# Delta-rule and linear-attention loops written out, with a new order of steps and a second set of statistics

## What is computed

```python
def _forward(x, ...):                       # one sequence: 512 x 256
    h = rmsnorm(layernorm(x) * ln1_g + ln1_b)
    q, k, v = (silu(causal_conv4(h @ W)) for W in (Wq, Wk, Wv))
    q, k = l2norm(q) * Kd ** -0.5, l2norm(k)
    g = -exp(A_log) * softplus(h @ Wa + dt_bias); beta = sigmoid(h @ Wb)
    # 4 heads, Kd = 64, Vd = 128, token after token:
    S = S * exp(g_t); S = S + k_t (x) ((v_t - k_t S) * beta_t); o_t = q_t S
    o = rmsnorm(o) * silu(h @ Wg)
    x = x + o @ Wo
    return gelu(layernorm(x) @ W2 + b2) + x
```

## Time and profile before

| what | us |
|---|---|
| runs of the kernel before | 4533.56, 4539.57, 4521.59 |
| median | 4533.56 |
| profiled execution | 4549.05 |
| its span | 4547.4 |
| TensorE, VectorE, ScalarE, GpSimd busy in the span | 3962.4, 2468.9, 1990.0, 1100.5 |

### The profile page before, as it was taken

The page is one execution under the profiler, slowest core; times in us unless marked ns, Lnnn a source line. Parts: engine busy times, 40 slices in busy tenths (PEclk is TensorE's granted clock), DMA queues, the critical chain, the costliest instruction groups (busy, mean ns, idle before and its releaser), DMA issues.

```text
span 4547.4 us, 72522 instructions
## 1 busy us (share of the span) xinstructions
PE 3962.4 (87%) x23860; PEld 3063.0 (67%) x23860; DVE 2468.9 (54%) x5456; ACT 1990.0 (44%) x4069; POOL 1100.5 (24%) x1686
## 2 busy tenths in 40 slices
PE   6888788598999999994798888888888888879998
PEld 3555555377888888883576666676676677756666
DVE  6888888452222222224577777777777777431111
ACT  5656555111212222122466666666666666432221
POOL 0111111101222222212334444443334343200000
PEclk8888889699999999997799999999999999889999
DMA  1010010254555555552111111111111110011111
GB/s 34 29 42 29 28 40 22 64 147 167 184 183 183 183 183 183 184 181 82 38 35 42 43 43 43 43 43 43 43 42 43 43 43 24 19 58 55 55 55 51
DMA packets 220956, 346.98 MB, mean 76 GB/s; under 512 B 99972, under 2 KB 171908, under 8 KB 202500
## 3 DMA queue, kind: packets, MB, share of 16 engines
q1 hardware_dynamic: 196932, 272.74, 18.9%
q0 software_dynamic: 23760, 71.07, 5.0%
HBM read 276.61 MB, written 68.16 MB: 76 GB/s over the span
## 4 chain that ended last, share of the span: by engine, by line
PE 23%; POOL 8%; issue 8%; DVE 8%; ACT 4%; DMA 2%; SPq 2%; POOLq 0%; DVEq 0%; ACTq 0%
PE gdr_bank L1320 5%; PE gdr_bank L1311 5%; DVE gdr_y L1729 3%; POOL gdr_vblk L1628 2%; PE gdr_bank L2363 2%; POOL gdr_tblk L1626 2%; PE gdr_bank L2375 1%; PE gdr_bank L2240 1%; PE gdr_bank L2359 1%; SPq L1519 1%; POOL gdr_ssq L1616 1%; PE gdr_bank L2408 1%; POOL gdr_orr L1616 1%; POOL gdr_got L1582 1%; POOL gdr_vblk L1623 1%
## 5 line engine op out<-in xcount | busy, mean ns | idle before, releaser
L525 ACT ACTIVATE moe_rel<-moe_fc 128x512 f32<-128x512 f32 x284 | 169.6, 597 | 798.5 <-PE moe_fc L490 798.5
L490 PE MATMUL moe_fc<-moe_xT,moe_win 128*128 128x256 f32 x2272 | 503.8, 380 | 1.5 <-issue 0.8
L501 PE MATMUL moe_o<-moe_wout,moe_hT 128*128 128x256 f32 x2272 | 502.0, 379 | 0.0
L490 PEld LDWEIGHTS moe_fc<-moe_xT,moe_win 128*128 128x128 f32 x2272 | 432.7, 191 | 61.2 <-issue 2.1
L501 PEld LDWEIGHTS moe_o<-moe_wout,moe_hT 128*128 128x128 f32 x2272 | 426.3, 190 | 55.1
L549 DVE TENSOR_TENSOR moe_hT<-moe_rel 128x512 f32<-128x512 f32 x284 | 196.6, 692 | 361.3 <-ACT moe_rel L525 361.3
L1729 DVE SCALAR_TENSOR_TENSOR gdr_y<-gdr_bank,gdr_cw,gdr_y 128x511 f32<-128x511 f32 (+2 forms) x384 | 287.5, 749 | 51.1 <-ACT gdr_y L2007 28.9
L2240 PE MATMUL gdr_bank<-gdr_hT,gdr_wqkv 128*128 128x512 f32 x512 | 263.6, 645 | 31.9 <-ACT gdr_qk L2022 26.8
L558 DVE COPY moe_osb<-moe_o 128x512 f32<-128x512 f32 x71 | 49.1, 692 | 424.9 <-PE moe_o L501 424.9
L2359 PE MATMUL gdr_bank<-gdr_ident,gdr_T 128*128 128x128 f32 x768 | 136.0, 306 | 109.7 <-DMA gdr_T<-blocks_in 95.0
L1311 PE MATMUL gdr_bank<-gdr_hT,gdr_wqkv 128*128 128x512 f32 x512 | 225.4, 599 | 3.5 <-ACT gdr_hT L1329 3.5
(11 more groups left out here) (391 smaller groups left out, 8843.1 us busy)
## 6 DMA issues: line engine op xcount, KB each, us to landing
moe_win<-in_moe_w SPq DMA_DIRECT2D x71, 1024.0 KB, 7.9
moe_wout<-in_moe_w SPq DMA_DIRECT2D x71, 1024.0 KB, 5.1
slots_out<-moe_osb POOLq DMA_DIRECT2D x71, 256.0 KB, 7.4
gdr_fz<-mixed_rows SPq DMA_DIRECT2D x18, 512.0 KB, 3.8
gla_xp<-in_xT_rows SPq DMA_DIRECT2D x16, 512.0 KB, 4.7
gla_xres<-in_x_rows SPq DMA_DIRECT2D x16, 512.0 KB, 3.9
token_rows<-gla_x POOLq DMA_DIRECT2D x16, 512.0 KB, 3.4
rt_W<-in_fc_b SPq DMA_DIRECT2D x32, 256.0 KB, 3.4
```

Of the source, the lines that this page charges most:

```text
L490: ins = nc.tensor.matmul(fc_ps[j][:, m % 2, :], win[u][:, c, m * P:(m + 1) * P], xT[:, c, :], start=(c == 0), stop=(c == DT - 1))
L501: ins = nc.tensor.matmul(o_ps[u][:, t, :], hT[u][:, k, t * P:(t + 1) * P], wout[u][:, k, :], start=(k == 0), stop=(k == FT - 1))
L525: nc.scalar.activation(rel[:, j, :, :], fc_ps[j][:], ACT.Relu).then_inc(relu_done, 1)
```

## The change

The hardware loops of linear attention (VectorE, ScalarE, TensorE) and of the delta rule (all five engines) are written out as Python loops over b=2 to 13, so that every body and period has its own instructions. The slot loops of VectorE, ScalarE and TensorE and `CHUNK_AT` go; each stream has its steps one under the other, in an order that differs in places:

- TensorE: chunk (0,2) ahead of `reach`; the rest of chunk (1,1) and all channel copies of half 1 ahead of `first_half(4,2)` (before: behind it).
- VectorE: `last_sum` from slot 2 to slot 9, between `rates(0)` and `rates(1)`; `last_norm` from slot 4 to slot 13, behind `merge(4,2)` and `merge(4,3)` and ahead of `norm3`; `conv(4)` behind `merge(4,0)` and `merge(4,1)` (before: ahead); the second scan of the second pair behind `merge(6,1)` (before: ahead of `merge(6,0)`).
- ScalarE: `gelu` from slot 0 to behind tap 4, ahead of the half copies of level 4, between `conv_silu(3)` and `conv_silu(4)`; `decay_keys`, `restart`, `squares` and the channel copies by a few places.
- GpSimd: the power for `last_sum` behind the second inversion. SyncE: `return_blocks(1)` ahead of the x3 store.
- `last_sum` and `last_norm` have a third set of `stats`, `agg`, `var` and `rstd`.

```diff
@@ VectorE, linear attention (ScalarE and TensorE alike) @@
-                with dve.Fori(0, (B - 4) // 2) as i:
-                    for u in range(2):
-                        body(i * 2 + 2 + u, u, i * 2 + 1 + u, True, i + 2)
+                for b in range(2, B - 2):
+                    body(b, b % 2, b - 1, True, b // 2 + 1)
@@ delta rule @@
-        stats, agg, var, rstd = ([sb(f"{n}{i}", [P, TT] + w) for i in range(2)]
+        stats, agg, var, rstd = ([sb(f"{n}{i}", [P, TT] + w) for i in range(3)]
...
-            with eng.Fori(0, (B - 4) // 2) as i:
-                for u in range(2):
-                    period(i * 2 + 2 + u, u, here=True, front=True, ln=True, past=True, end=True)
+            for b in range(2, B - 2):
+                period(b, b % 2, here=True, front=True, ln=True, past=True, end=True)
@@ GpSimd @@
-                    if end:
-                        power(b - 2, var[1][:], rstd[1][:], "tl_var", 2, "tl_rstd", TT)
...
                     if here:
                         invert_blocks(1, b)
+                    if end:
+                        power(b - 2, var[2][:], rstd[2][:], "tl_var", 2, "tl_rstd", TT)
@@ VectorE, the new order (conditions left out) @@
+                        merge(4, 0, b)
+                        merge(4, 1, b)
+                        conv(4, b + 1)
...
+                        scan(2, b)
+                        merge(6, 0, b)
+                        merge(6, 1, b)
+                        scan(3, b)
+                        key_decays(1, b)
...
+                        rates(0, b + 1)
+                        last_sum(b - 2)
+                        rates(1, b + 1)
...
+                        merge(4, 2, b)
+                        merge(4, 3, b)
+                        last_norm(b - 2)
+                        norm3(b - 1)
@@ ScalarE, the new order (conditions left out) @@
+                        conv_silu(3, b + 1)
+                        tap(4, b + 1)
+                        gelu(b - 2)
+                        half_level(4, 0, b)
+                        half_level(4, 1, b)
+                        spread_out(3, b + 1)
+                        conv_silu(4, b + 1)
+                        tap(5, b + 1)
+                        half_level(5, 0, b)
+                        half_level(5, 1, b)
@@ TensorE, the new order (conditions left out) @@
+                        channels(0, (0, 1), b + 1)
+                        chunk(1, 0, b, u)
+                        channels(0, (2,), b + 1)
+                        channels(1, (0,), b + 1)
+                        chunk(1, 1, b, u)
+                        channels(1, (1, 2), b + 1)
+                        first_half(4, 2, b)
+                        first_half(4, 3, b)
+                        second_half(4, 2, b)
```

More of the change, by code:

```diff
@@ L1900, in last_norm @@
                     wait("tl_rstd", 2)
-                    done("x3", 1, row_scale(nc, n1, x3, agg[1], rstd[1], TT))
+                    done("x3", 1, row_scale(nc, n1, x3, agg[2], rstd[2], TT))
                 def period(b, u, here=False, front=False, ln=False, past=False, end=False):
                     w = 1 - u
[L1905 to L1968, removed]
-                            decay(b + 1, w)
-                            values_beta(0, b + 1, w)
-                        if slot == 13 and ln:
-                            rms(0, b + 2)
-                        if slot == 14 and front:
-                            values_beta(1, b + 1, w)
-                        if slot == 14 and ln:
-                            rms(1, b + 2)
-                        if slot == 15 and past:
-                            bias(1, b - 1)
@@ new lines, in period @@
+                    if ln:
+                        norm2(b + 2)
+                    if here:
+                        merge(4, 2, b)
+                        merge(4, 3, b)
+                    if end:
+                        last_norm(b - 2)
+                    if past:
+                        norm3(b - 1)
+                    if not later(b, -1) and front:
+                        dve.wait_ge(ready, 1)
+                    if front:
+                        decay(b + 1, w)
+                        values_beta(0, b + 1, w)
@@ new lines, in period @@
+                    if ln:
+                        rms(0, b + 2)
+                    if here:
+                        chunk(1, 2, b, u)
+                        merge(5, 2, b)
+                        merge(5, 3, b)
+                    if front:
+                        values_beta(1, b + 1, w)
+                    if ln:
+                        rms(1, b + 2)
+                    if front:
+                        scan(0, b + 1)
+                        scan(1, b + 1)
+                    if past:
+                        bias(0, b - 1)
@@ L1980, in _ @@
+                    if here:
+                        merge(6, 2, b)
+                        merge(6, 3, b)
+                    if past:
+                        bias(1, b - 1)
+                loop(period)
                 fc_vector(dve)
@@ L2503, in _ @@
-                loop(pe, period)
+                    if past and here:
+                        pe.wait_ge(s["DT"], b * TT + 2)
+                    if past:
+                        chunk(2, 0, b - 1, w)
+                    if here and past:
+                        pe.wait_ge(s["Uf"], b * TT)
+                    if here and end:
+                        pe.wait_ge(s["yb"], (b - 1) * 2)
+                    if here:
+                        key_products(0, b, u)
+                    if front:
+                        project(0, b + 1)
+                        project(1, b + 1)
@@ new lines, in period @@
+                    if past:
+                        chunk(2, 1, b - 1, w)
+                    if past and here:
+                        pe.wait_ge(s["qd"], b * TT + 2)
+                    if past and end and not here:
+                        pe.wait_ge(s["yb"], (b - 1) * 2)
+                    if past:
+                        gate(0, b - 1)
+                        chunk(2, 2, b - 1, w)
+                    if front:
+                        to_tokens(0, b + 1)
+                    if past:
+                        gate(1, b - 1)
@@ new lines, in period @@
+                    if past:
+                        for c in range(1, DH):
+                            mix_out(c, b - 1)
+                    if here:
+                        chunk(0, 1, b, u)
+                        chunk(0, 2, b, u)
+                    if front and not later(b, -1):
+                        pe.wait_ge(ready, 1)
+                        pe.wait_ge(aprep, 3)
+                    if front:
+                        reach(b + 1)
+                        channels(0, (0, 1), b + 1)
```

516 lines of the change are left out of this document (313 added, 203 removed).

## The result

The changed kernel took 4576.46 us (median of 5 runs, 4564.70 to 4581.67), the kernel before 4533.56: a ratio of 1.0091, 95% interval 1.0063 to 1.0118. That is 43 us slower where 56 us faster was forecast.

A forecast was written before the change was run, and what follows sets the result against it. VectorE's order paces linear attention; TensorE is mostly busy in the delta rule, with some 160 us of waits. Linear attention -27, periods -27, prologue and tail -2: -56 from 4533.6 gives 4478 us, range 4438 to 4520.

The forecast's parts named there:

- Loops, linear attention: Twelve linear-attention bodies written out lose the loop jump and cost 564 us instead of 591.2: -27 us, bounds -34 to -21.
- Loops, delta rule: Delta rule: unrolling alone takes the period from 115.25 to 111.0 us, -55 us over thirteen periods; other end -14.
- Rival (c): Straight code waits for instructions as the jump did, so linear attention stays: 4534 to 4562 us, chance 0.06.
- First half, the stall: Delta rule, first half: late convolution 4 and an added table load delay TensorE's copy: +3.3 us, bounds +2.3 to +5.1.
- First half, the sum: Delta rule, first half of a period: 52.3 - 0.9 - 1.1 + 3.3 = 53.6 us, between 50.3 and 55.7.
- rival (b): Slower: ScalarE's queue stalls the first half and slow stretches follow; period 121.4, 4585 us, chance 0.09.
- The other terms: First half: 52.3 us written out, -0.9 for earlier inverted blocks, -1.1 for the earlier block copy that L2344 awaits.
- ScalarE's table load: One more load a period, before convolution 4's SiLU: 1.28 us; the skill page's cost would give 4496 us.
- Second half: Delta rule, second half of a period: 58.7 - 1.0 + 1.9 = 59.6 us, between 57 and 61.
- The last norm's price: Second half: the norm in slot 13, ahead of VectorE's path to the merge, adds +1.9 us, bounds 0 and 3.
- Last sum out of the first half: First pair's block inversion, freed of the last sum, gives its blocks earlier: -0.9 us a period, bounds 0 and -1.2.
- Prologue and tail: Already straight code, these get the new order alone: -2 us by the same -0.9 and -1.0 in a few periods.

The follow-up runs named there:

- both edits back: The changed kernel with GELU and convolution 4 put back in their old places: 4460.3 us, ratio 0.9849 to the kernel before.

## Why the prediction was wrong

**Loops, linear attention (-27 forecast).** Right in kind, and too large: -18.5, short of the 21 that was the least by the bounds. Straight bodies cost 47.7 us, more than either bound (46.43 and 47.48); the one straight body of the trace before was no measure for the twelve.

**Loops, delta rule (-55 by unrolling alone).** Right in kind, and too large: the kernel with only its loops written out has a period of 112.1 for the 111.0 forecast, so the thirteen periods gained 41 us of the 55. With linear attention the forecast has 82 us for writing out, and 55 were measured. The first half was right (52.4 for 52.3); the second is 59.7 on average, not the 58.7 of the one straight period it was read from. Rival (c), straight code waiting for its instructions, falls.

**First half, the stall (+3.3).** The mechanism, place and length were right: 3.36 us, convolution 4 behind the merges, a fifth table load, the copy behind both.

**First half, the sum (53.6).** This is the step that failed: the term +3.3 for the stall. The forecast took the stall's length as its price and kept the half-speed stretch for the upper bound, though the earlier trace rows showed such a stretch after a wait of 3.90 us, and the change was to make another of 3.3. There it got 2.1 us (55.7), where rival (b) put 3.3 on the same stretch. The runs put 8.0 us on the stall (57.7 against 49.7 with both edits back), and 4.2 of them are the clock, since with the idle time filled the half is 53.5. The other terms held in sum: 52.3 - 0.9 - 1.1 = 50.3 was forecast without the stall, and 49.7 came. The changed kernel's first half is 57.7, 4.1 us over the forecast and 2.0 over its upper bound. 4.1 x 13 = 53 us, over half of the 99 by which the median was missed. Rival (b) named this with its price (121.4 a period, 4585 us; 118.4 and 4576.5 came) and had a chance of 0.09.

**ScalarE's table load.** The forecast took 1.28 us from the row; the Trainium skill, "ScalarE: Activation LUTs", section "What ACT_TABLE_LOAD costs", counts some 2.7 us with the drain. The trace of the changed kernel doesn't agree: from the start of the load at 2901.21 to the next activation is 1.30 us, at 2910.97 too. That one more load stands in each period did cost, but only in the queue behind the late convolution: taking it away there gave 58 us, and with convolution 4 early the wait was 0.27 to 0.45 us with the load still in place.

**Second half (59.6).** It came out at 60.7, 1.1 over, 14 us in all. What the order adds was right in sum: +0.9 forecast (-1.0 and +1.9), and 60.7 against the 59.7 of the loops alone; in part by luck, since the last sum cost 2.1 there by its own run, not 0.9. The base of 58.7 was too low by 1.0. The wait for the solved blocks is 1.9 on average for the 1.8 forecast. The last norm's price is 1.7 in the second half by its own run, 1.3 in the period, for the 1.9 of the sum; it does not come as a steady wait, but as 1.65 us in some periods with a slow stretch behind some of these.

**Last sum out of the first half (-0.9).** The two runs that differ by it put 2.0 us on the first half, more than forecast, and about as much back on the second; as a move it was neutral, not a gain.

**Prologue and tail (-2).** The period ahead of the thirteen rose from 109.0 to 115.4 us (2219.11 to 2334.54). The span after the thirteen periods fell from 705.6 (3841.77 to 4547.4) to 695.4 us (3873.56 to 4569.0): together -4. No run shows that the order did either. With the loops alone written out, where prologue and tail are as before, the span after the periods is 696.1 us too; with the new order and the loops kept, the period ahead is 108.9.

**The profiled execution.** The one before was 15.5 us over its median, the one after is 5.9 under: by the spans the loss is 21.6 us, by the medians 43. The rest of the 99 lies here (21), in linear attention (8.5) and in its start, which came 4.8 us later in this execution and not in the other kernels with the same code there.

## What to carry to other kernels

Price a wait of TensorE by what follows it: where a trace shows a half-speed stretch behind a wait of some length, give a predicted wait of that length both prices, its own and that of the stretch, here 3.4 us and 4.2. It need not come each time: behind 3.36 us it came in twelve of twelve first halves, behind 2.08 us in seven of twelve. Before moving a step to a place where its engine is idle, look at what is queued behind it and at the table it leaves for the next step. Test a loop's removal and a new order apart: here the one was worth 55 us and the other cost more than that, and only together did they look like a small loss.

## What the runs showed of the hardware

Doing more can be faster: 2.8 us of useless matmuls a period made the kernel 52 us faster, since the granted clock stayed at 1.00 where it had been 0.59. The stretch at half speed after the unfilled wait cost 4.2 us, more than the wait of 3.36.

Two edits whose single effects are 58 and 84 us give 110 together, as both work on the same wait; the size of one was not to be had from the other.

The two halves did not reach full clock together. With both edits back the first half ran at full clock in 49.7 us, while its second half stayed at 61.3 with a clock of 0.91. With the last sum and the last norm in the first half again, the first half took 52.1 us at 0.98 and the second 57.5 at 0.97, and that kernel was the fastest.
